# Relative rows of four heads from one product with block-diagonal tables, in an attention kernel for one core

## The reference, cut to what matters

```python
Rh = _rel_lookup(rel_pos_h, H)          # (32, 32, 16)
Rw = _rel_lookup(rel_pos_w, W)
r_q = q.reshape(B * nh, H, W, hd)
rel_h = jnp.einsum('bhwc,hkc->bhwk', r_q, Rh)
rel_w = jnp.einsum('bhwc,wkc->bhwk', r_q, Rw)
attn = (attn.reshape(B * nh, H, W, H, W) + rel_h[:, :, :, :, None]
        + rel_w[:, :, :, None, :]).reshape(B * nh, H * W, H * W)
attn = jax.nn.softmax(attn, axis=-1)
```

## Time and profile before

| | |
|---|---|
| time, median of 3 runs | 7709.82 us (7704.64 to 7717.52) |
| the profiled execution's own time | 7721.76 us |
| its span in the profile | 7720.1 us |
| PE busy | 6859.2 us, 89% |
| DVE busy | 5270.4 us, 68% |
| ACT busy | 3702.7 us, 48% |
| POOL busy | 1969.9 us, 26% |

### The profile page before, as it was taken

The page is one execution under the profiler, slowest core; times in us unless marked ns, Lnnn a source line. Parts: engine busy times, 40 slices in busy tenths (PEclk is TensorE's granted clock), DMA queues, the critical chain, the costliest instruction groups (busy, mean ns, idle before and its releaser), DMA issues. The chain is left out here.

```text
span 7720.1 us, 152771 instructions
## 1 busy us (share of the span) xinstructions
PE 6859.2 (89%) x54592; PEld 4058.6 (53%) x54592; DVE 5270.4 (68%) x7775; ACT 3702.7 (48%) x6761; POOL 1969.9 (26%) x2311
## 2 busy tenths in 40 slices
PE   3999999999877989479999999997786799999998
PEld 2555555555455555245555555553332455555555
DVE  3666666666566788546666666664978677777776
ACT  0444444444522554224444444443011677777777
POOL 3335344344220000043443434431111000000000
PEclk7998999999987888679899999998676899999999
DMA  6776776776459878477677677672221555555553
GB/s 160 162 146 126 148 148 125 145 144 130 86 184 223 137 118 123 111 167 148 131 142 149 124 145 149 130 138 79 86 80 65 144 129 142 125 135 136 125 141 92
DMA packets 500291, 1025.76 MB, mean 133 GB/s; under 512 B 80103, under 2 KB 276392, under 8 KB 460280
## 3 DMA queue, kind: packets, MB, share of 16 engines
q1 hardware_dynamic: 452406, 932.06, 55.3%
q0 software_dynamic: 47360, 86.53, 7.1%
HBM read 670.93 MB, written 358.93 MB: 133 GB/s over the span
## 5 line engine op out<-in xcount | busy, mean ns | idle before, releaser
L1468 DVE TENSOR_REDUCE a_nmp<-a_S 128x2 f32<-128x1024 f32 x1536 | 1877.7, 1224 | 988.5 <-PE a_S L1325 973.6
L1605 ACT ACTIVATE a_PROB<-a_T 128x512 f32<-128x512 f32 x3072 | 1667.2, 595 | 1678.2 <-PE a_T L1304 1661.5
L1197 POOL CAST a_RF<-a_RL 32x512 fp32r<-32x512 f32 x1536 | 1299.6, 846 | 378.6 <-DVE a_RL L1521 289.4
L2350 DVE CUSTOM_DVE_ANT_0 a_X<-a_S,a_mask 128x1024 f32<-128x1024 f32 x768 | 921.2, 1219 | 414.9 <-PE a_S L2260 409.2
L1338 PE MATMUL a_O<-a_PROB,a_V 128*32 128x512 f32 x6144 | 951.3, 696 | 0.5 <-ACT a_PROB L1605 0.5
L2410 ACT ACTIVATE a_PROB<-a_T 128x512 f32<-128x512 f32 x1536 | 833.9, 599 | 208.4 <-PE a_T L2274 203.1
L1300 PEld LDWEIGHTS a_T<-a_QW,a_KW 64*128 64x128 f32 x3072 | 301.0, 189 | 1143.7 <-issue 1137.8
L1300 PE MATMUL a_T<-a_QW,a_KW 64*128 64x512 f32 x3072 | 804.8, 518 | 70.0 <-ACT a_PROB L1605 69.9
L2274 PE MATMUL a_T<-a_ident,a_X 128*128 128x128 f32 x6144 | 832.0, 278 | 4.1
L2274 PEld LDWEIGHTS a_T<-a_ident,a_X 128*128 128x128 f32 x6144 | 666.1, 141 | 274.0 <-issue 261.7
L1325 PEld LDWEIGHTS a_S<-a_KV,a_QV 64*128 64x128 f32 x6144 | 649.7, 203 | 136.7 <-issue 0.2
(11 more groups left out here) (166 smaller groups left out, 8676.4 us busy)
## 6 DMA issues: line engine op xcount, KB each, us to landing
a_QV<-a_part_rows SPq DMA_DIRECT2D x384, 256.0 KB, 7.4
a_rel_rows<-a_RF SPq DMA_DIRECT2D x96, 1024.0 KB, 9.1
a_K<-part_rows SPq DMA_DIRECT2D x576, 128.0 KB, 4.0
a_part_rows<-a_part SPq DMA_DIRECT2D x48, 1024.0 KB, 15.8
a_QV<-a_part_rows SPq DMA_DIRECT2D x384, 128.0 KB, 7.9
a_QV<-a_rel_rows SPq DMA_DIRECT2D x384, 128.0 KB, 7.5
a_QW<-a_rel_rows SPq DMA_DIRECT2D x192, 256.0 KB, 8.9
a_mask<-L_mask SPq DMA_DIRECT2D x48, 1024.0 KB, 6.7
```

Source lines behind the costliest of these rows:

```text
L1197: nc.gpsimd.tensor_copy(dst, src).then_inc(permuted, 1)
L1468: nc.vector.tensor_reduce(nmp[:, qh, c, 2 * pr:2 * pr + 2, kh], S[:, pr], AX.X, ALU.max).then_inc(s_done, 1)
L1605: nc.scalar.activation(PROB[:, s % PRING, 2 * pr + sd], T[:, slot(("st", s, pr, sd))], ACT.Exp).then_inc(t_act, 1)
L2350: nc.vector.tensor_tensor_reduce(out=X[:, v % 2, c, g], in0=S[:, sd].rearrange("p a b -> p (a b)"), in1=mask[:, n % 2, g, c], scale=1.0, s ...
```

## The change

The tables are laid out block-diagonally over the four heads: 64 rows (four heads of 16 channels), and for each position 128 columns (32 keys of each of four heads, the head as the last index). One product of such a table with the queries of one image row or column, straight from the first 64 partitions of `whole`, gives the relative rows of all four heads. `rel0` and `rel1` are the row terms of the two halves, `rel2` and `rel3` the column terms. Each is 16 products with 64 rows and 128 columns of stationary data and 32 moving columns.

`QC`, its four transfers, `permute` and `RF` are gone. ACT and DVE write straight into `RL`, which now holds a whole unit; for the column terms they write with a stride of 32 elements. `store_tables` waits for DVE's last `rel` piece and stores `RL` with eight transfers, each of 32 partitions four apart. ACT's wait for `permuted` becomes a wait, at `rel0` alone, for the stores of the unit before. The tables loaded at the start of a layer are sixteen times as large for the column terms (1 MB), and the one subtraction that makes `tab_d` covers four times the elements in a partition.

```diff
-        QC = sb("QC", [DIM, G, TOKENS])
-        RL = [sb(f"RL{i}", [P, 2, BANK], F32R) for i in range(2)]
-        RF = sb("RF", [P, 2, G, BANK], F32R)
+        RL = sb("RL", [P, 2, 2, TOKENS], F32R)
...
-        tab_h = sb("tab_h", [DIM, 2 * SIDE - 1])
-        tab_w = QC[:, 0].rearrange("p (x c) -> p x c", c=SIDE)
-        tab_d = sb("tab_d", [DIM, SIDE, SIDE])
+        tab_h = sb("tab_h", [G * DIM, (2 * SIDE - 1) * G])
+        tab_d = sb("tab_d", [G * DIM, SIDE, SIDE, G])
+        tab_w = PROB[0:G * DIM].rearrange("p r g t -> p (r g t)").rearrange("p (x c g) -> p x c g", c=SIDE, g=G)
...
+        def table_lines(r, i):
+
+            way, part_ = divmod(r, 2)
+            if way == 0:
+                return RL[:, 0, i, part_ * BANK:(part_ + 1) * BANK]
+            return RL[:, 1, i].rearrange("p (y x) -> p x y", x=SIDE)[:, 16 * part_:16 * part_ + 16]
+
+        def table_bank(r, to):
+            return T[:, to] if r < 2 else T[:, to].rearrange("p (x y) -> p x y", y=SIDE)
...
-            def lines(v, ready):
-
-                sp.wait_ge(t_dve, ready)
-                alone(sp)
-                for g in range(G):
-                    sp.dma_start(QC[:, g], whole[DIM * g:DIM * g + DIM]).then_inc(qc_moved, 16)
...
-            def store_tables(v, par):
-                sp.wait_ge(permuted, MOVES * (v + 1))
+            def store_tables(par, ready):
+                sp.wait_ge(t_dve, ready)
                 alone(sp)
-                for half in range(2):
-                    sp.dma_start(rel_rows[par, half], plain(RF[64 * half:64 * half + 64])).then_inc(rel_stored, 16)
+                for way in range(2):
+                    for g in range(G):
+                        sp.dma_start(rel_rows[par, way, g], plain(RL[g:P:G, way])).then_inc(rel_stored, 16)
...
-                if more:
-                    for r in range(4):
-                        permute(u + 2, r, upto(u, f"rel{r}", "dve"))
...
-            def relative(v, r, to):
-                pe.wait_ge(qc_moved, 64 * (v + 1))
+            def relative(r, to, ready):
+                pe.wait_ge(t_dve, ready)
                 alone(pe)
-                for a in range(8):
-                    for half in range(2):
-                        x = 8 * r + a
-                        at = 64 * half
-                        last = nc.tensor.matmul(T[at + 32:at + 64, to, 64 * a:64 * a + 64], tab_d[:, x],
-                                                QC[:, :, half * BANK + x:(half + 1) * BANK:SIDE], start=True, stop=True)
-                        if a < 4:
-                            i = 16 * half + 4 * r + a
-                            nc.tensor.matmul(T[at:at + 32, to, P * a:P * a + P],
-                                             tab_h[:, SIDE - 1 - i:2 * SIDE - 1 - i],
-                                             QC[:, :, SIDE * i:SIDE * i + SIDE], start=True, stop=True)
+                way, part_ = divmod(r, 2)
+                for a in range(16):
+                    x = 16 * part_ + a
+                    if way == 0:
+                        table, queries = tab_h[:, G * (SIDE - 1 - x):G * (2 * SIDE - 1 - x)], whole[0:G * DIM, SIDE * x:SIDE * x + SIDE]
+                    else:
+                        table, queries = tab_d[:, x].rearrange("p c g -> p (c g)"), whole[0:G * DIM, x:TOKENS:SIDE]
+                    last = nc.tensor.matmul(T[:, to, SIDE * a:SIDE * a + SIDE], table, queries, start=True, stop=True)
                 last.then_inc(t_ready, 1)
...
-                    ins = nc.vector.tensor_tensor(RL[1][:, r % 2], T[:, to], plain(RL[0][:, r % 2]), ALU.subtract)
+                    ins = nc.vector.tensor_tensor(table_lines(r, 1), table_bank(r, to), plain(table_lines(r, 0)), ALU.subtract)
...
-                    need(act, permuted, MOVES * v + 8 * (r - 1), solo=True)
-                    ins = nc.scalar.copy(RL[0][:, r % 2], T[:, to])
+                    if r == 0:
+                        need(act, rel_stored, TABLES * v, solo=True)
+                    ins = nc.scalar.copy(table_lines(r, 0), table_bank(r, to))
```

More of the change, by code:

```diff
@@ L1143, in opening @@
                 query_rows(1, 1, 0)
-                store_tables(1, 1)
-                sp.wait_ge(rel_stored, 64)
+                store_tables(1, begun("rel3", 1, "dve"))
+                sp.wait_ge(rel_stored, 2 * TABLES)
                 alone(sp)
@@ L1179, in separate @@
                                         ).then_inc(split, 1)
-            def permute(v, r, ready):
-                pool.wait_ge(t_dve, ready)
-                if r == 0:
-                    need(pool, rel_stored, 32 * v)
-                    pool.wait_ge(split, SPLITS * (v + 1))
-                alone(pool)
-                for i in range(2):
-                    for quad in range(4):
-                        lines = slice(32 * quad, 32 * quad + 32)
-                        if quad % 2 == 0:
-                            src = RL[i][lines, r % 2].rearrange("p (i g x) -> p i g x", g=G, x=SIDE)
-                            dst = RF[lines, i].rearrange("p g (i x) -> p i g x", x=SIDE)[:, 4 * r:4 * r + 4]
-                        else:
-                            src = RL[i][lines, r % 2].rearrange("p (x g y) -> p x g y", g=G, y=16)
-                            dst = RF[lines, i].rearrange("p g (y x) -> p x g y", x=SIDE)[:, 8 * r:8 * r + 8]
-                        nc.gpsimd.tensor_copy(dst, src).then_inc(permuted, 1)
             def store(b, half, m, ready):
@@ L1205, in place @@
             def place(v, par):
-                need(pool, permuted, MOVES * (v + 1) if not isinstance(v, int) or v else 0)
                 pool.wait_ge(t_dve, begun("v1", v, "dve") if isinstance(v, int) and v < 2 else upto(v - 2, "v1", "dve"))
@@ L1237, in _ @@
                     separate(v, half, begun(f"qk{half}", v, "dve"))
-                for r in range(4):
-                    permute(v, r, begun(f"rel{r}", v, "dve"))
             for hg in range(GROUPS):
@@ L1513, in take @@
                     half = int(n[2])
-                    need(eng, qc_moved, 64 * v)
+                    if half == 0 and not (isinstance(v, int) and v == 0):
+                        eng.wait_ge(t_ready, begun("rel3", v - 1, "pe") if isinstance(v, int) and v < 3
+                                    else upto(v - 3, "rel3", "pe"))
                     need(eng, split, SPLITS * v)
@@ L1541, in prologue @@
                 eng.wait_ge(consts_loaded, CONSTS)
-                nc.vector.tensor_tensor(tab_d[:], tab_w, tab_w[:, :, 0:1].to_broadcast([DIM, SIDE, SIDE]),
+                nc.vector.tensor_tensor(tab_d[:], tab_w, tab_w[:, :, 0:1].to_broadcast([G * DIM, SIDE, SIDE, G]),
                                         ALU.subtract).then_inc(set_up, 1)
-                nc.vector.tensor_copy(part[0:DIM, 0], QC[:, 1]).then_inc(set_up, 1)
+                nc.vector.tensor_copy(part[0:DIM, 0], ones_h).then_inc(set_up, 1)
                 nc.vector.tensor_copy(KW[:], whole[:]).then_inc(set_up, 1)
@@ L2499, in _spread_heads, with _block_of_each @@
     return z.reshape(w.shape[:-1] + (P,))
+def _block_of_each(t):
+    z = np.zeros((G,) + t.shape + (G,), t.dtype)
+    for g in range(G):
+        z[g, ..., g] = t
+    return z.reshape((G * DIM,) + t.shape[1:] + (G,))
 def _turn_pairs(w):
@@ L2566, in _layouts @@
             rw = inp[f"L{i}_conv_rel_pos_w"][::-1].T
-            a[p + "tab_h"] = rh
-            a[p + "tab_w"] = np.stack([rw[:, SIDE - 1 - x:2 * SIDE - 1 - x] for x in range(SIDE)], axis=1)
+            windows = np.stack([rw[:, SIDE - 1 - x:2 * SIDE - 1 - x] for x in range(SIDE)], axis=1)
+            a[p + "tab_h"] = _block_of_each(rh).reshape(G * DIM, -1)
+            a[p + "tab_w"] = _block_of_each(windows)
             a[p + "bvb"] = np.broadcast_to(by(bv)[:, None, :], (GROUPS, P, G * DIM))
```

29 lines of the change are left out of this document (12 added, 17 removed).

## The result

The changed kernel takes 8042.53 us in the median of four runs (8041.6 to 8068.01), the kernel before 7712.8 us beside it: a ratio of 1.0437, 95% interval 1.0414 to 1.0459. The forecast was 8107 us. The profiled execution took 8043.34 us by its own time, of which 8041.7 us are its span; that of before took 7721.76.

A forecast was written before the change was run, and what follows sets the result against it. PE was taken to bound the kernel (busy 89%). 7721.8 + 260 (burst) + 137 (clock) + 0 = 8118.6 us for the profiled execution; the runs' median, 11.9 lower, gives 8107 us, 5.1% slower. Whole range 7740 to 8290.

The forecast's parts named there:

- the likeliest case: Whole kernel: longer bursts and a clock that still falls, 8107 us, own range 7920 to 8255; chance 0.65.
- The burst: PE's rel jobs in bodies: 32 records at 0.112 us, 3.57 us instead of 2.09; +1.48 us a job, +260 us.
- The clock: Rel jobs in bodies: clock falls at least once a job; middle of one slow stretch (+0) and two (+275): +137 us.
- The rival of the clock that holds: Clock stays at 1.00 behind rel bursts, so slow stretches go; 7655 us, faster; chance 0.15.
- The argument from the old burst: Against the holding clock: PE was busy 2.10 of 2.10 us in the old burst, yet the clock fell.
- Shorter loads: Rival: rel loads 0.08 us a record, one slow stretch a job as now; 7793 us; chance 0.12.
- A clock that stays down: Rival: more than two slow stretches a rel job, say three; 8519 us; chance 0.04.
- POOL and transfers: In the bodies, removed reordering copies gain 0, as nobody on the path waits; two more issues on SP's queue cost 0.
- Evictions: ACT's and DVE's strided column writes still end in time: 0; at full clock up to 0.7 us a job.
- The prologue: Start of each of two layers: waits go, larger table and longer bursts come; 0, with -25 to +5 us each.

The follow-up runs named there:

- wide_moving: Changed kernel with 64 instead of 32 moving columns in each relative product, same loads (relative rows wrong data); 7717.69 us, ratio 1.0022 to the kernel before.
- narrow_loads_2: Changed kernel with each product in the bodies loading only 32 of the 128 table columns (three heads' values missing); 7385.22 us, ratio 0.9589 to the kernel before.
- after_in_eight: Changed kernel with its rel work in eight pieces of 8 products at steps 5 to 12, same products; 7622.11 us, ratio 0.9894 to the kernel before.
- copies_back: Changed kernel with the old narrow products, reading four heads from `QC`, its four copies and their wait restored; 7683.85 us, ratio 0.9965 to the kernel before.
- plain_evictions: Changed kernel with column terms written without the stride, so their order in `RL` differs; 8056.02 us, ratio 1.046 to the kernel before.

## Why the prediction was right, and where it was off

**Sign and size.** 8107 forecast, 8042.5 measured, within the likeliest case's own range. The mechanism held: wider loads set a longer burst, next to nothing covers it, the clock still falls, and POOL's relief is worth next to nothing. The sum for the profiled execution was 8118.6 - 8043.3 = 75 us too high: 33 by the burst, 21 by the clock, 11 by the other steps of a unit and 10 by the prologues, as follows.

**The burst, predicted +1.48 us a job and 260 us.** The pace was right (0.112 us a record predicted, 0.112 measured), its translation into a step was not. A step with a row job at full clock goes from 3.22 + 2.12 = 5.34 us to (414.78 - 410.58) + (417.21 - 414.78) = 6.63, which `wide_moving` shows as well. That is +1.29 us, or 227 us for 176 jobs. I had set the whole 32 x 0.112 against the old 2.09 us and allowed for no overlap; at 414.78 the scores' first load and matmul start ahead of the last two of the burst, and this half of the step grows by only 0.98 us. 0.31 us come back in the half behind it (2.43 us for 2.12), which I had left unchanged. The Trainium skill, "TensorE: Matmul & The Clock Gate", section "LDWEIGHTS (loading the stationary operand)", has a load cost its columns divided by 1.2 in ns, an estimate of 107 ns for 128 columns; this trace agrees at full clock with 0.112 us, and `wide_moving` and `narrow_loads_2` show that the load is the pace.

**The clock, predicted +0.78 us a job and 137 us.** Over all 176 jobs the two halves of a job's step take 8.76 us on the mean, against 6.81 before (6.90 in the job of the earlier trace rows, which I had taken for all): +1.95 us, 343 us in all. Less the 227 of the burst, 116 us are left for the clock, 0.66 us a job. Slow time gives the same: it grows from 13.2 to 18.4 us a unit, and 44 x 5.2 us at half the clock lose 114 us. So the size was near, but the picture behind it was not. I had the clock fall once a job at least, with one slow stretch or two behind it. 35 of 176 jobs passed with both halves at full clock, and of the 141 slow stretches in the bodies 96 last 6.8 us, where nearly all lasted 3.4 before; others ran their burst partly at 0.50 and the scores behind it too, as at 420.5. That the middle between two bounds, which no row gave, came within 21 us is luck in part.

**The rival of the clock that holds, 0.15.** It did not come, but `wide_moving` shows how near it was: the same loads with 64 moving columns would have done it, and so did half the burst (`after_in_eight`). The argument from the old burst, that to be busy was not enough, is confirmed: PE is busy for 2.20 of 2.20 us in the burst in which the clock falls at 420.5, and for 6.60 of 6.60 in `wide_moving`, where it holds. In the changed kernel's prologue it is busy for 13.80 of 13.80 us in the `rel` bursts from 115.00 to 128.80, at 0.50 throughout. The rule of the Trainium skill that I had named there, same page, "What's actually happening", read as the share of time in which PE is busy, would have led wrong.

**Shorter loads, 0.12: wrong.** At full clock the records were 0.112 us apart, not 0.08. That this is because they all use the same 64 rows was my reason, and no run tests it. **A clock that stays down: wrong.**

**POOL and transfers, predicted 0.** `copies_back` gives -25 us for all of it with the prologues. POOL fell to 672 us where I said 612; its copies had been shorter in the bodies than in the prologue. No wait of PE for rows came in the bodies.

**Evictions, predicted 0, at full clock up to 0.7 us.** ACT's column copies take 1.06 us for 0.58 and DVE's 1.09 for 0.69, and `plain_evictions` shows no time for them: PE waits only in the 19 column jobs at full clock, 8.4 us in all. `wide_moving`, at full clock, shows the bound: 0.5 us for each column job.

**The prologue, predicted 0, from -25 to +5.** The last piece came at 165.04 for 171.15. The first `transposed` of layer 0 starts 5.8 us earlier than before (198.39 for 204.15), that of layer 2, counted from the end of the norm ahead, 3.9 us. Several things nearly cancelled. The waits on copies and POOL went; the first value projections began 7.9 us later (100.15 for 92.22), behind the larger table and its subtraction, for which I had 7; and four bursts of 64 records took 11.4 to 13.8 us each, where they were at the low clock at 0.21 us a record.

**The sum.** From its first to its last `transposed`, the body of layer 0 takes 158 us longer and that of layer 2 174, 332 together. The jobs' steps account for 343, so the other steps give back 11; why is not shown. Less 10 for the prologues that makes 322, of 321.6 between the two executions.

## What to carry to other kernels

Count a weight load by its columns, and ask what streams behind it: merging narrow products into wide ones saves nothing where each load then outlasts its few moving columns. Price a burst at both clocks and by the whole step around it, for how long it is can decide more than its work: the same products in halves, one a step, were 5% faster. And where work is cut up, look whose queue must now deliver earlier: eight pieces lost 2% on SP's queue and gained 1.4% on POOL's.

## What the runs showed of the hardware that was not expected

- Under the same loads of 128 columns the clock fell with 32 moving columns (unit mean 0.89) and held at 1.00 with 64 (7718 us against 8043). With 32 moving columns it held too when the load was 32 columns wide (bursts of 1.20 and 1.98 us), or the burst half as long.
- The order in which a moving operand's columns lie changes both a burst (2.13 against 1.92 us) and the clock behind it (13.2 against 3.6 us of slow time a unit), with one head's values in both kernels: 7682 against 7499 us. Under loads of 32 columns a burst whose moving columns lie 32 elements apart took 1.98 us, one with 32 side by side 1.20.
- A write of 512 values a partition with a stride of 32 elements costs ACT 1.06 us for 0.59. DVE, which also reads one of its inputs with that stride, takes 1.09 for 0.69.
- A load and its matmul may start ahead of others that the program issues before them: at 414.78 the scores' first load and matmul come before the burst's last two loads (414.86 and 414.97) and matmuls (414.89). Why they can is not shown.
